# The first unit of a graph layer: its loads on two queues, its layer norm on GpSimd, its products piece by piece

## The reference

```
h = maximum(layernorm(x), 0)                  # eps 1e-5, no gain
def conv(x, a, eps, W, b):
    ax = a @ x
    h = ax + (1 + eps[0]) * ax
    for i in range(3):
        h = relu(h @ W[i].T + b[i])
    return h
out1 = conv(h,  adj, eps1, W1, b1)
out2 = conv(x2, adj, eps2, W2, b2)
return x + concatenate((out1, out2), 1) @ Wm.T + bm
```

## Time and profile before

| | before |
|---|---|
| median of 3 runs | 408.82 us |
| the profiled execution | 408.38 us |
| its span | 406.9 us |
| PE busy | 402.3 us (99%), 1774 matmuls |
| DVE, ACT busy | 219.5 us, 220.2 us (54% each) |
| POOL busy | 30.2 us |
| granted TensorE clock | 1.00 over the whole span |

### The profile page before, as it was taken

One profiled execution on the slowest core, in us unless ns is written; L12 is line 12 of the kernel. 1 busy time (PEld: TensorE's weight loads), 2 busy tenths in 40 slices (PEclk: granted clock), 3 DMA queues, 4 the chain that ended last, 5 costly groups with the idle time before them and its releaser, 6 DMA issues.

```text
span 406.9 us, 4872 instructions
## 1 busy us (share of the span) xinstructions
PE 402.3 (99%) x1774; PEld 328.7 (81%) x1774; DVE 219.5 (54%) x260; ACT 220.2 (54%) x259; POOL 30.2 (7%) x35
## 2 busy tenths in 40 slices
PE   8999999999999999999999999999999999999996
PEld 3888888888888888888888888888888888888886
DVE  5888887655455334551645517445373444755223
ACT  5876667658474623555434556334565335766034
POOL 1223332100000000000100001000000000000100
PEclk9999999999999999999999999999999999999999
DMA  7998785744645174235584336653175550840100
GB/s 259 423 404 308 304 317 208 254 186 132 232 180 176 58 258 184 106 132 200 149 315 152 114 146 231 233 206 130 77 258 206 206 198 35 270 170 0 52 2 26
DMA packets 14317, 76.21 MB, mean 187 GB/s; under 512 B 1952, under 2 KB 2208, under 8 KB 6368
## 3 DMA queue, kind: packets, MB, share of 16 engines
q1 hardware_dynamic: 12960, 71.97, 47.4%
q0 software_dynamic: 1200, 3.93, 3.0%
q10 hardware_dynamic: 144, 0.13, 0.1%
HBM read 73.93 MB, written 2.10 MB: 187 GB/s over the span
## 4 chain that ended last, share of the span: by engine, by line
PE 99%; DVE 0%; issue 0%; DVEq 0%
PE acc L510 25%; PE acc L506 25%; PE acc L507 25%; PE second_acc L506 3%; PE second_acc L510 3%; PE second_acc L507 3%; PE hidden L507 3%; PE hidden L506 3%; PE hidden L510 3%; PE merged L514 2%; PE merged L507 1%; PE merged L506 1%; PE merged L510 1%; PE acc L534 0%; PE acc L549 0%; PE acc L544 0%
## 5 line engine op out<-in xcount | busy, mean ns | idle before, releaser
L506 PE MATMUL acc<-adj_hi,feat_lo 128*128 128x512 f32 x440 | 171.8, 390 | 0.0
L510 PE MATMUL acc<-adj_lo,feat_hi 128*128 128x512 f32 x440 | 171.7, 390 | 0.0
L507 PE MATMUL acc<-adj_hi,feat_hi 128*128 128x512 f32 x440 | 171.1, 389 | 0.0
L376 DVE TENSOR_TENSOR adj_lo<-adj_raw,adj_hi 128x2048 fp32r<-128x2048 f32 x48 | 108.3, 2288 | 37.9 <-ACT adj_hi L243 36.9
L243 ACT ACTIVATE adj_hi<-adj_raw 128x2048 fp32r<-128x2048 f32 x48 | 90.4, 1926 | 17.6 <-PE acc L510 15.8
L382 DVE TENSOR_TENSOR act_lo<-act_f,act_hi 128x512 fp32r<-128x512 f32 x60 | 41.0, 690 | 105.6 <-ACT act_f L263 105.6
L507 PEld LDWEIGHTS acc<-adj_hi,feat_hi 128*128 128x128 f32 x440 | 82.6, 188 | 17.7
L510 PEld LDWEIGHTS acc<-adj_lo,feat_hi 128*128 128x128 f32 x440 | 82.6, 188 | 17.8
L506 PEld LDWEIGHTS acc<-adj_hi,feat_lo 128*128 128x128 f32 x440 | 82.6, 188 | 17.3
L262 ACT ACTIVATE act_hi<-hidden,bias 128x512 fp32r<-128x512 f32 x45 | 31.0, 688 | 96.2 <-PE hidden L510 96.2
L438 DVE TENSOR_TENSOR adj_lo<-adj_raw,adj_hi 128x2048 fp32r<-128x2048 f32 x14 | 31.7, 2290 | 7.8 <-ACT adj_hi L284 7.8
(11 more groups left out here) (76 smaller groups left out, 238.0 us busy)
## 6 DMA issues: line engine op xcount, KB each, us to landing
adj_raw<-adj_tiles SPq DMA_DIRECT2D x62, 1024.0 KB, 5.1
x_rows<-x_tiles SPq DMA_DIRECT2D x16, 256.0 KB, 6.9
adj_raw<-adj_first SPq DMA_DIRECT2D x8, 256.0 KB, 5.1
x_res<-x_t POOLq DMA_DIRECT2D x8, 256.0 KB, 6.3
out_t<-y_sb POOLq DMA_DIRECT2D x7, 256.0 KB, 2.3
w_raw<-w_t SPq DMA_DIRECT2D x1, 512.0 KB, 5.8
out_t<-y_sb SPq DMA_DIRECT2D x1, 128.0 KB, 1.8
out_t<-y_sb ACTq DMA_DIRECT2D x1, 128.0 KB, 1.8
```

The source lines that it names most:

```text
L376: nc.vector.tensor_tensor(adj_lo[:, u % RING, :], adj_raw[:, u % RING, :], f32(adj_hi[:, u % RING, :]), ALU.subtract).then_inc(lo_made, 1)
L506: nc.tensor.matmul(out, lhs_lo, rhs_hi, start=start, stop=False)
L507: nc.tensor.matmul(out, lhs_hi, rhs_hi, start=False, stop=False)
L510: return nc.tensor.matmul(out, lhs_hi, rhs_lo, start=False, stop=stop)
```

## The change

SP no longer issues x2 and x of unit 0. ACT issues them from its own queue as its first two instructions, and SP starts with the first tile of `adj`. The first tile keeps its four pieces; the second comes in two pieces of 128 x 1024 instead of four. Before SP issues the loads of unit 1 it waits until the second piece of the first tile has landed.

The scaling of the layer norm of unit 0 moves from ACT to Pool, four instructions with `rstd` and `shift`; ACT then makes `feat_hi` of branch 0 with one relu, between the first and the second tile's `adj_hi`, and Pool makes its own relu before it subtracts. The other units keep the old way.

On PE the eight products of zeros inside the first tile are gone. Branch 1 of a first tile now takes all three products of a piece in turn as they come ready, and the order of the first two tiles is by tile: s = 0 for branch 1, s = 0 for branch 0, then s = 1 for both.

```diff
-    FINE_LOADS = 2
-    FINE_SIGNALS = JB - 1
+    PIECES = ((1, 1, 1, 1), (2, 2))
-    FILLERS = 2
@@ sync
             for s, (u, c) in enumerate(OPENING):
-                if c == 0:
+                if s == len(PIECES):
+                    sp.wait_ge(fine_loaded[1], 16)
+                if c == 0 and s > 0:
                     load_x2(u)
                     load_x(u)
-                if s < FINE_LOADS:
-                    for j in range(JB):
-                        cols = slice(j * CW, (j + 1) * CW)
-                        done = fine_loaded[s * FINE_SIGNALS + j] if j < FINE_SIGNALS else raw_loaded[s]
-                        sp.dma_start(adj_raw[:, s, cols], adj_first[s * JB + j]).then_inc(done, 16)
+                if s < len(PIECES):
+                    source = (adj_first, adj_second)[s]
+                    for i in range(len(PIECES[s])):
+                        js, n = piece(s, i)
+                        cols = slice(js.start * CW, js.stop * CW)
+                        done = raw_loaded[s] if n is None else fine_loaded[n]
+                        sp.dma_start(adj_raw[:, s, cols], source[i]).then_inc(done, 16)
@@ gpsimd
+            low_of_x2(0)
+            pool.wait_ge(x_loaded[0], 16)
+            pool.wait_ge(rstd_made, 1)
+            for j in range(JB):
+                last = nc.gpsimd.tensor_scalar(x_rows[:, 0, j, :], x_rows[:, 0, j, :], rstd[:, j:j + 1],
+                                               shift[:, j:j + 1], ALU.mult, ALU.add)
+            last.then_inc(first_norm_made, 1)
+            pool.wait_ge(feat1_hi_made, 1)
+            nc.gpsimd.tensor_scalar(x_rows[:, 0], x_rows[:, 0], 0.0, None, ALU.max).then_inc(first_relu_made, 1)
+            pool.wait_ge(first_relu_made, 1)
+            nc.gpsimd.tensor_tensor(feat_lo[:, 0, 0:JB, :], x_rows[:, 0], f32(feat_hi[:, 0, 0:JB, :]),
+                                    ALU.subtract).then_inc(feat1_lo_made, 1)
@@ scalar
+            act.dma_start(x2_rows[:, 0], x2_tiles[0]).then_inc(x2_loaded[0], 16)
+            act.dma_start(x_rows[:, 0], x_tiles[0]).then_inc(x_loaded[0], 16)
             act.wait_ge(zeros_made, 1)
             nc.scalar.activation(root_of_zero[:, :], zeros[:, 0:1], ACT.Sqrt)
-            for u in range(U - 2):
+            high_of_x2(0)
+            std_of_x(0)
+            high_of_opening(0)
+            act.wait_ge(first_norm_made, 1)
+            nc.scalar.activation(feat_hi[:, 0, 0:JB, :], x_rows[:, 0], ACT.Relu).then_inc(feat1_hi_made, 1)
+            high_of_opening(1)
+            for u in range(1, U - 2):
                 high_of_x2(u)
                 std_of_x(u)
@@ tensor, pieces_aggregate(s, b), for the first branch
+                    for i in parts:
+                        n = piece(s, i)[1]
+                        if n is None:
+                            pe.wait_ge(hi_made, s + 1)
+                        else:
+                            pe.wait_ge(fine_hi_made, n + 1)
+                        add(feat_hi, adj_hi, i)
+                        if i == 0:
+                            pe.wait_ge(feat2_lo_made, u + 1)
+                        add(feat_lo, adj_hi, i)
+                        if i > 0:
+                            low_ready(i - 1)
+                            add(feat_hi, adj_lo, i - 1)
+                    low_ready(parts[-1])
+                    add(feat_hi, adj_lo, parts[-1])
@@ tensor, the order
-            for s in range(0, len(OPENING), 2):
+            for at in range(len(PIECES)):
+                for b in BRANCH_ORDER:
+                    pieces_aggregate(at, b)
+            for s in range(2, len(OPENING), 2):
```

More of the change, by code:

```diff
@@ L160, in f32, with piece @@
             return ap.bitcast(F32)
+        def piece(s, i):
+            at = sum(PIECES[s][:i])
+            return range(at, at + PIECES[s][i]), (None if i == len(PIECES[s]) - 1
+                                                  else sum(len(p) - 1 for p in PIECES[:s]) + i)
         def quarter(q):
@@ L216, in _, with low_of_x2 @@
         def _(pool):
-            for u in range(U):
+            def low_of_x2(u):
                 rows = slice(u * JB, (u + 1) * JB)
@@ L268, in operand, with piece_high @@
                     branch_operand(m, k, b)
[L270 to L272 removed]
+            def piece_high(s, i):
+                js, n = piece(s, i)
+                cols = slice(js.start * CW, js.stop * CW)
+                act.wait_ge(raw_loaded[s] if n is None else fine_loaded[n], 16)
                 nc.scalar.activation(adj_hi[:, s, cols], adj_raw[:, s, cols], ACT.Copy).then_inc(
[L274 removed]
+                    hi_made if n is None else fine_hi_made, 1)
             def high_of_opening(s):
[L277 to L279 removed]
+                if s < len(PIECES):
+                    for i in range(len(PIECES[s])):
+                        piece_high(s, i)
                     return
@@ L521, in opening_bank, with pieces_aggregate @@
                 return (second_acc if c else acc)[b]
[L523 removed]
+            def pieces_aggregate(s, b):
                 u, c = OPENING[s]
                 out = opening_bank(c, b)
[L527 to L551 removed]
@@ new lines, in pieces_aggregate, with add, low_ready @@
+                parts = range(len(PIECES[s]))
+                def add(feat, adj, i):
+                    for j in piece(s, i)[0]:
+                        slot, cols = columns(s, j)
+                        last = nc.tensor.matmul(out[:, :], feat[:, b, u * JB + j, :], adj[:, slot, cols],
+                                                start=(u == 0 and j == 0 and feat is feat_hi and adj is adj_hi), stop=False)
+                    return last
+                def low_ready(i):
+                    n = piece(s, i)[1]
+                    if n is None:
+                        pe.wait_ge(lo_made, s + 1)
+                    else:
+                        pe.wait_ge(fine_lo_made, n + 1)
@@ new lines, in pieces_aggregate @@
+                pe.wait_ge(feat2_hi_made if b else feat1_hi_made, u + 1)
+                if b == first:
+                    for i in parts:
+                        n = piece(s, i)[1]
+                        if n is None:
+                            pe.wait_ge(hi_made, s + 1)
+                        else:
+                            pe.wait_ge(fine_hi_made, n + 1)
[8 more added lines that the diff above has]
+                    add(feat_hi, adj_lo, parts[-1])
+                else:
+                    for i in parts:
+                        add(feat_hi, adj_hi, i)
+                    for i in parts:
+                        add(feat_hi, adj_lo, i)
+                    pe.wait_ge(feat1_lo_made, u + 1)
+                    for i in parts:
+                        last = add(feat_lo, adj_hi, i)
+                    signal(u, b, last)
@@ L632, in _ @@
             pe.wait_ge(zeros_made, 1)
-            idle_products(WARM_UP)
-            for s in range(0, len(OPENING), 2):
+            for _ in range(WARM_UP):
+                nc.tensor.matmul(merged[:, :], zeros[:, 0:P], zeros[:, :], start=True, stop=True)
+            for at in range(len(PIECES)):
+                for b in BRANCH_ORDER:
+                    pieces_aggregate(at, b)
+            for s in range(2, len(OPENING), 2):
                 for b in BRANCH_ORDER:
                     for at in (s, s + 1):
-                        if at < FINE_LOADS:
-                            fine_aggregate(at, b)
-                        else:
-                            opening_aggregate(at, b)
+                        opening_aggregate(at, b)
                     if s == len(OPENING) - 2:
```

58 lines of the change are left out of this document (21 added, 37 removed).

## The result

The changed kernel takes 412.15 us (median of 6 runs, 412.09 to 412.26), the kernel before 408.62 us (6 runs, 408.29 to 409.11). The ratio is 1.0089, 95% interval 1.0078 to 1.0100: slower by 3.5 us. The profiled execution took 412.26 us with a span of 410.0, against 408.38 and 406.9: 3.9 more, of which 3.1 in the span. (The profiled execution of the kernel before lies 0.2 under its median, so the medians differ by less.) Each run lists its span beside its time; over the runs the median of time less span is 2.13 after and 1.50 before. So about 0.6 us lie outside the span.

The account below looks back on a forecast made before the run. PE's gapless row of matmuls from 7.08 us was the bound, `adj_lo` of s = 2 the one deadline. The profiled 408.4 plus 3.1 for that `adj_lo` coming late gave 411.5, put at 411.6; range 408.0 to 413.6.

Parts of the forecast that it names:

- Products of zeros: PE, first tile: removal gains up to 1.8 us, capped at 1.0 by `adj_lo` of s = 2, if that is no later.
- X: Start of DVE's statistics on x of unit 0: from 4.40 to 5.25 us, x landing third; bounds 4.40 to 6.9.
- The rival of even sharing: ACT's and SP's queues share evenly, x lands fourth at 6.9 us: 413.2 us in all; chance 0.13.
- Statistics to shift: DVE statistics, root, `rstd` and `shift` of unit 0: 2.73 us from X, so `shift` at 8.0.
- The scaling: Pool's four scalings: 0.30 us each (0.17 to 0.40), taking turns with DVE's four `adj_lo`, both done at 11.8.
- ACT behind the wait: ACT's relu to `feat_hi` waits for Pool, ends at 12.5 us; the second tile's two `adj_hi` at 13.5 and 14.5.
- Pool's relu and subtraction: Pool after the scaling: relu 0.75 us (0.63 to 1.29), subtraction 1.29, done at 14.6, holding off DVE's `adj_lo`.
- The second tile's last `adj_lo`: DVE: ends at 17.0 us, or 18.3 if Pool's subtraction for x2 of unit 1 goes first; both carried on.
- PE not later: PE before s = 2: finishes the second tile at 20.2 to 21.5 us, no later than `adj_lo` of s = 2.
- Faster: Rival: Pool's scaling not held up, x lands by 4.8 us, `adj_lo` of s = 2 at 19.42: 407.4 us; chance 0.15.
- no change: Rival: Pool free or little held up, x late (5.3 to 6.5), cancelling the zeros' gain: around 408.5 us; chance 0.20.
- the clock: Rival: PE's idle stretches of about 1 us lower its clock, costing 2.7 us more: about 414; chance 0.03.

Follow-up runs that it names:

- e5: Kernel before with the eight products of zeros inside the first tile taken out, nothing else: 407.97 us, ratio 0.9989.
- e7: As e6, but scaling of unit 0 on DVE ahead of its first `adj_lo`, and `feat_lo` of x on DVE: 408.93 us, ratio 1.0009 to before.
- e10: As e9, with the tile of s = 2 loaded, split and multiplied in two pieces: 407.72 us, ratio 0.9982 to before.
- e1: Kernel before with only x2 and x of unit 0 issued from ACT's queue: 409.75 us, ratio 1.0034.
- e8: As e1, but x issued ahead of x2 on ACT's queue: 409.10 us, ratio 1.0013 to before.
- e4: Changed kernel with DVE waiting for Pool's four scalings before its first `adj_lo`: 413.46 us, one run.
- e2: Changed kernel with the loads of x2 and x of unit 0 given back to SP, ahead of `adj`: 410.61 us, ratio 1.0053 to before.
- e3: Changed kernel with the scaling of unit 0 on ACT between the two tiles' `adj_hi`; Pool only subtracts: 409.82 us, ratio 1.0035 to before.
- e6: Changed kernel with both the loads back on SP and the scaling of unit 0 on ACT: 409.01 us, ratio 1.0014 to before.
- e11: Kernel before plus one scratch scaling behind Pool's last first-phase work and a memset at the start: 408.78 us, ratio 1.0010.
- e9: As e7, with the first tile's 24 products on PE in another order: 408.76 us, ratio 1.0003 to before.
- e12: Kernel before with the second tile's blocks passed as an input of their own: 408.26 us, ratio 0.9993.

## Why the prediction was right

The forecast was 411.6 for 412.15, slower, and the mechanism is in the main the one it named: Pool and DVE in turn, ACT standing behind Pool for 2.64 us, `adj_lo` of s = 2 late. The wait of about 2 us on PE for that `adj_lo`, which it named as a sign, did not come, since PE was late itself: 0.25 is left of it. Point by point:

- *Products of zeros.* Nothing was won from them, as expected, since s = 2 is late. But "gain up to 1.8, capped at 1.0" was wrong for the old order. e5 shows 0.2: most of the zeros stood in waits for ACT's `adj_hi`, and `feat_hi` of branch 0 comes next. The sum took a row without gaps for a row that could be shortened, and its cap looked at one deadline, where three lie. With PE's new order and early `feat_hi` more was won: the End of e7 came 0.6 ahead. That of e10 came 1.3 ahead, past the cap, because it splits s = 2 itself.
- *The two loads, X.* Put at 5.25 (x third), measured 6.03. This is the mis-sized term, by 0.78. The rival of even sharing named the right mechanism and a price too high (6.9, 413.2): the queues' transfers land in pairs, but the issues also come earlier, 1.43 instead of 2.39 for the fourth. e1 and e8 show it twice more. The Trainium skill (DMA: Bandwidth & Descriptors, Queues, rings and completion order) has each DMA engine take packets from its queues in turns. By that rule the traces agree: the landings are 3.6 and 3.7, then 4.4 and 4.6 us after the issue.
- *Statistics to shift.* X + 2.73 was taken; `shift` ends at 8.76, X + 2.73.
- *The scaling.* Taken at 0.30, measured 0.44, past the upper bound of 0.40. Done at X + 6.5 by the sum, at 12.45 = X + 6.4 by the trace; DVE's four were not slowed at all, and the extra 0.6 of scaling was covered by an overlap of the same size. That Pool waits for DVE's `adj_lo` is shown by e4. Here too the rows bear out the rule of the Trainium skill that was weighed (SBUF — State Buffer, Who interferes with whom), for a Pool instruction with a single tensor input as well. But Pool's first scaling stood through three `adj_lo`, not only through the one that had been issued first.
- *ACT behind the wait.* The relu ended at 13.11 for 12.5, the two `adj_hi` at 15.0 for 14.5: X again.
- *Pool's relu and subtraction.* Taken to 14.6, measured to 16.51. The relu took 1.49 for 0.75, and it is past its bound of 1.29. For the first 0.96 of the 1.49 DVE stood still, in e2 too, so at least part of the excess is the instruction's own; no run has it alone.
- *The second tile's last `adj_lo`.* 17.0 or 18.3 was left open; it ended at 17.59, which is the first of the two plus the late X, less 0.2. DVE went ahead of Pool's subtraction for x2. The turns came otherwise than in the sum: DVE's first of this tile was not held (1.23), its second was (2.29 for 1.22), by Pool's subtraction for x. So X came out 0.78 above, the order 0.65 below the middle. The total of 3.1, for 3.25 measured at the third product of s = 2, was met by two errors that cancel, which is luck and not precision. From DVE's next statistics to `adj_lo` of s = 2 took 5.9 for 5.85.
- *PE not later.* This is the step that failed. By the sum branch 0's last four would end at 15.5 and the second tile at 20.2 to 21.5; they ended at 17.76 and 23.21, since Pool's `feat_lo` was 1.9 late. It cost next to nothing only because DVE's side was as late (23.43).
- *Outside the span.* Taken as before, 1.5, measured 2.13, and no step of the prediction had the difference. Counted from End, 0.5 is lost (5.47 for 4.95); e2 and e4 lose it too (5.50, 5.39), e1, e3 and e6 do not, so it comes with Pool's scaling and relu. How is open (e11 finds about 0.3). It is of the size by which the time lies above the forecast, 0.5.
- *Faster, no change, the clock.* Pool was held up and x came at 6.0, against both. The granted clock stayed at 1.00 in the changed kernel; in e4, with a wait of 1.9 at this place, it came down.

The 3.5 us, by the runs: 1.4 to 1.5 from the loads (e1; after less e2), 1.6 from Pool's scaling and relu (e2 less e6, the loss after End included), 0.6 from the rest of the order (e6). Taken off in the other order, it is 2.2 for Pool's part (after less e3) and 0.9 for the loads (e3 less e6).

## What to carry to other kernels

In these traces a transfer that a first chain of small instructions needs is not made earlier by a queue of its own when another queue starts beside it: it shares, and the second of each queue lands with the second of the other. Work on one tile belongs on the engine that will not have to share with the next engine's long instructions, even if it is the busier one: DVE did in 1.1 us what Pool, idle but in DVE's way, did in 3.5. When filler work is taken off a gapless engine, ask first whether it stands in a wait, then look for all deadlines behind it, on both operands; the gain is the smallest slack.

## What the runs showed that was not expected

- Time less span is not a constant of this kernel: 1.50 before, 1.73 with two loads on ACT's queue, 2.13 to 2.20 with Pool's scaling and relu, 1.95 in e7, e9 and e10. Over one kernel's runs it scatters by 0.1 to 0.4. By itself it is no cost: in e1, e3, e6 and e8 the span only ended sooner after End, and time less End stayed at 4.94 to 5.03 for 4.95. With Pool's scaling and relu time less End grew too, by 0.4 to 0.55. A further input does not explain it (e12), a memset and a scaling on Pool explain about 0.3 (e11). The rest is open.
- The last stores, issued the same way in all kernels, land in 1.8 us when the end is at 403.2 or later, and in 2.8, 2.4 and 2.3 in e7, e9 and e10, whose end is earlier. Why was not tried.
- The clock fell to 1.2 GHz in e4 after one stretch of 1.9 us, with four products and an earlier wait of 0.8 in front of it, and not in the changed kernel after two stretches of 1.3 us.
